# Key units by context half, rounding copies on ScalarE, and NF4 chunks placed 1-8-3 around the attention heads

## The reference

```
def nf4_quant_dequant(w):             # blocks of 64 along a row
    absmax = max(abs(block)); normalized = block / absmax
    idx = searchsorted(bounds, normalized)        # 15 bounds, 16 codes
    return NF4_CODE[idx] * absmax
x = x + attention(layernorm(x), ctx, ctx, mask, Wq, Wk, Wv, Wo)
    # 32 query heads, 8 key/value heads of 128, rotary positions on q and k,
    # logits = 30 * tanh(q k / sqrt(128) / 30), softmax over 128 keys
dq1, dq2, dq3 = (nf4_quant_dequant(w) for w in (w1, w2, w3))   # 1376x512, 1376x512, 512x1376
h = silu(layernorm(x) @ dq1.T) * (layernorm(x) @ dq2.T)
x = x + h @ dq3.T
```

## Time and profile before

| | us |
|---|---|
| median of 3 runs (893.6 to 898.36) | 896.76 |
| the profiled execution | 898.33 |
| its span | 896.4 |
| TensorE busy | 819.5 (91%) |
| VectorE busy | 706.8 (79%) |
| ScalarE busy | 439.3 (49%) |
| GpSimd busy | 467.9 (52%) |

### The profile page before, as it was taken

One profiled execution on the slowest core, in us unless ns is written; L12 is line 12 of the kernel. 1 busy time (PEld: TensorE's weight loads), 2 busy tenths in 40 slices (PEclk: granted clock), 3 DMA queues, 4 the chain that ended last, 5 costly groups with the idle time before them and its releaser, 6 DMA issues.

```text
span 896.4 us, 10644 instructions
## 1 busy us (share of the span) xinstructions
PE 819.5 (91%) x3806; PEld 650.7 (73%) x3806; DVE 706.8 (79%) x793; ACT 439.3 (49%) x521; POOL 467.9 (52%) x272
## 2 busy tenths in 40 slices
PE   3688799899899999899999899999767999998998
PEld 3566587677677778677777677777546788887886
DVE  8798968589888988788888788988887799895120
ACT  0044466466565566555665565565642365462100
POOL 3445437865965955846856847857321335444000
PEclk9899999899999999999999999999989999999999
DMA  8454564632433432522523423422201311303210
GB/s 322 135 156 144 158 202 107 195 113 67 115 113 82 149 83 71 171 60 71 162 74 89 146 63 91 147 71 58 81 1 32 103 48 54 106 1 103 56 59 36
DMA packets 61941, 91.82 MB, mean 102 GB/s; under 512 B 6721, under 2 KB 28353, under 8 KB 61889
## 3 DMA queue, kind: packets, MB, share of 16 engines
q1 hardware_dynamic: 61888, 91.14, 34.6%
HBM read 51.00 MB, written 19.14 MB: 78 GB/s over the span
## 4 chain that ended last, share of the span: by engine, by line
PE 52%; DVE 17%; POOL 13%; DMA 7%; issue 6%; ACT 4%; SPq 2%; POOLq 0%; DVEq 0%; ACTq 0%
POOL qT L1120 6%; PE bank L449 5%; PE bank L450 5%; PE bank L451 5%; PE bank L536 4%; DMA sw<-cs_loop 4%; PE bank L469 3%; PE bank L467 3%; PE bank L468 3%; PE bank L483 3%; PE bank L484 3%; PE bank L485 3%; PE trp L456 3%; PE avp L547 3%; DVE nfa L848 2%
## 5 line engine op out<-in xcount | busy, mean ns | idle before, releaser
L848 DVE SCALAR_TENSOR_TENSOR nfv<-nfp,nfv 128x1408 f32<-128x1408 uint8 x70 | 139.6, 1994 | 24.5 <-ACT nfp L681 22.7
L1120 POOL TENSOR_TENSOR qT<-cs_loop,sw 128x512 f32<-128x512 f32 x58 | 90.5, 1560 | 107.1 <-DMA sw<-cs_loop 102.1
L730 ACT ACTIVATE eb<-bank 128x512 f32<-128x512 f32 x64 | 38.3, 598 | 188.2 <-PE bank L536 188.2
L848 DVE SCALAR_TENSOR_TENSOR nfa<-nfp,nfa 128x1408 f32<-128x1408 uint8 x56 | 104.0, 1857 | 25.0 <-ACT nfp L681 24.4
L1185 POOL TENSOR_TENSOR eb<-eb,maskf 128x512 f32<-128x512 f32 x64 | 91.8, 1435 | 52.1 <-ACT eb L732 52.1
L681 ACT ACTIVATE nfp<-nfv,bnd 128x1408 uint8<-128x1408 f32 x75 | 106.9, 1460 | 14.3 <-DVE nfa L848 9.1
L483 PE MATMUL bank<-woh,ath 128*128 128x512 f32 x256 | 109.5, 428 | 0.0
L681 ACT ACTIVATE nfp<-nfa,bnd 128x1408 uint8<-128x1408 f32 x75 | 106.5, 1461 | 5.6 <-POOL nfa L1136 3.1
L467 PE MATMUL bank<-xh,wqh 128*128 128x512 f32 x256 | 106.8, 417 | 0.0
L848 DVE SCALAR_TENSOR_TENSOR nfx<-nfp,nfx 128x1408 f32<-128x1408 uint8 x42 | 83.7, 1992 | 25.2 <-ACT nfp L681 25.2
L484 PE MATMUL bank<-wol,ath 128*128 128x512 f32 x256 | 102.6, 401 | 0.0
(11 more groups left out here) (130 smaller groups left out, 1835.6 us busy)
## 6 DMA issues: line engine op xcount, KB each, us to landing
sw<-cs_loop SPq DMA_DIRECT2D x116, 128.0 KB, 2.3
stage<-wq_pieces SPq DMA_DIRECT2D x32, 256.0 KB, 2.9
stage<-wo_pieces SPq DMA_DIRECT2D x32, 256.0 KB, 2.9
stage<-dq_scratch SPq DMA_DIRECT2D x32, 256.0 KB, 3.2
sw<-cs_start SPq DMA_DIRECT2D x44, 128.0 KB, 2.4
ks_scratch<-qT SPq DMA_DIRECT2D x16, 256.0 KB, 2.5
vs_scratch<-vst SPq DMA_DIRECT2D x16, 256.0 KB, 3.3
kcur<-ks_scratch SPq DMA_DIRECT2D x16, 256.0 KB, 3.7
```

The source lines that it names most:

```text
L848: op = nc.vector.scalar_tensor_tensor(acc[:, :], nfp[:, n % 2, :], STEPS[i], acc[:, :], ALU.mult, ALU.add)
L1120: nc.gpsimd.tensor_tensor(dst, products(ru, slot)[:, 0, :], sw[:, slot, :], ALU.add).then_inc(roped, 1)
```

## The change

Five things change together.

1. Key units run over all eight key heads for the first half of the tokens, then for the second (`half, kv = u // 8, u % 8`), and Wk comes by head, so that key unit 0 needs piece 0 and context pieces 1 to 4 and starts with the first two; key units 1 to 7 need one piece more each.
2. The casts of pieces 0 to 27 are made by ScalarE (`first_hi`). VectorE and GpSimd share the low halves anew (`FIRST_POOL`). The six first groups of token transposes stand after key units 10 to 15, two after value units 0 and 1.
3. One chunk (the first quarter of w3) is made in value units 0 to 12, eight in the heads, three (45 steps) in hidden units 2 to 21 and behind them. w3 is cut by columns (`W3_RUNS`), so that early tiles of the down product need early chunks only.
4. The cast `hh` goes to ScalarE (`hidden_hi`), for unit n-1 after the silu of n.
5. The down product waits for the hidden low halves tile by tile.

```diff
@@ sync @@
-            for n in range(12):
+            for n in range(5):
                 first_piece(n)
+            sp.dma_start(tab[:, :, :], table_d).then_inc(tab_in, 16)
             sp.dma_start(mt8[:, :], mask_t).then_inc(mask_in, 16)
...
             for v in range(16):
-                if v == 4:
-                    nf_load(nf_first[:, CH:2 * CH], 1)
+                if v == 13:
+                    nf_load(1)
+                if v == 14:
+                    nf_store(0)
                 if v == 5:
-                    nf_store(dq3[:, 0:CH], 0)
...
+            sp.wait_ge(nf_out, nf_stored(NKV))
+            nf_load(NKV + 2)
             for n in range(4, 2 * HT):
-                if n == 14:
-                    nf_load(nf_first[:, 4 * CH:5 * CH], 11)
-                if n == 16:
-                    nf_store(dq3[:, 2 * CH:3 * CH], 10)
+                if n == 15:
+                    nf_store(NKV + 1)
+                if n == 17:
+                    nf_load(NKV + 3)
                 weights_in(n)
@@ tensor @@
+                half, kv = u // 8, u % 8
+                if u > 0:
+                    split(pe, 5 + u if half == 0 else 16)
...
+                for k in range(KT):
+                    if u == 0:
+                        split(pe, k + 2)
...
-                if n == 0:
-                    pe.wait_ge(h_lo, 2 * HT)
+                pe.wait_ge(h_lo, units_of(n))
@@ scalar @@
+            for n in range(16):
+                first_hi(n)
+            for u in range(10, NK):
+                first_token_hi(u - 10)
+                if u >= 12:
+                    first_hi(u + 4)
...
+                if v < 2:
+                    first_token_hi(6 + v)
+                for n in range(20 + 2 * v, 22 + 2 * v) if v < 4 else ():
+                    first_hi(n)
+                for i in nf_values(v):
+                    nf_above_bound(0, i)
...
                 silu(n)
-                chunk, bounds = nf_ffn(n)
-                for i in bounds:
-                    nf_above_bound(chunk, i)
+                if n > 0:
+                    hidden_hi(n - 1)
+                for c, i in nf_ffn(n):
+                    nf_above_bound(NKV + 1 + c, i)
+            hidden_hi(2 * HT - 1)
+            for c, i in nf_ffn(2 * HT):
+                nf_above_bound(NKV + 1 + c, i)
@@ vector @@
             for u in range(NK):
                 rope_parts(u, u % 2, tab[:, 0:2, :])
-                if u < 2:
-                    first_piece(12 + 2 * u)
-                    first_piece(13 + 2 * u)
+                if u < 6:
+                    first_low(5 + 2 * u)
...
-                for i in nf_keys(u):
-                    nf_add(0, i)
...
-                dve.wait_ge(h_done, n + 1)
-                nc.vector.tensor_copy(hh[:, t, half * 512:(half + 1) * 512], hf[:, n % 2, :]).then_inc(h_hi, 1)
...
+                if n in (1, 7, 14):
+                    nf_prepare(NKV + 1 + n // 7)
+                for c, i in nf_ffn(n):
+                    nf_add(NKV + 1 + c, i)
+            for c, i in nf_ffn(2 * HT):
+                nf_add(NKV + 1 + c, i)
@@ gpsimd @@
+                for n in {0: (8,), 2: (10,), 3: (12,), 5: (14,), 12: (16,), 13: (18,)}.get(u, ()):
+                    first_low(n)
-                if u == 2:
+                if u == 5:
                     power(0, range(B))
...
+            first_low(20)
+            nf_normalise(0)
+            for n in (22, 24, 26):
                 first_low(n)
...
+                if u == 3:
+                    nf_rescale(0)
+            nf_normalise(1)
...
-                if n in (1, 10):
-                    nf_normalise(10 + n // 10)
-                if n in (9, 18):
-                    nf_rescale(10 + n // 18)
+                if n in (1, 7, 14):
+                    nf_normalise(NKV + 1 + n // 7)
+                if n in (9, 16):
+                    nf_rescale(NKV + 1 + n // 16)
+            nf_rescale(NKV + 3)
```

More of the change, by code:

```diff
@@ L122, in build @@
         sb("ffn_place", [128, 6144])
+        with ExitStack() as ffn:
+            nfy = sb("nfy", [128, CH], f32, ffn)
         woh1 = sb("woh1", [128, G, D], f32r)
@@ L198, in split @@
         def split(eng, n):
-            if isinstance(n, int) and n <= WO0:
-                wait(eng, piece_lo, (n + 1) // 2)
-                wait(eng, piece_lo_dve, n // 2)
+            if n <= WO0:
+                early_pool = len([m for m in range(n) if m in FIRST_POOL])
+                wait(eng, piece_lo, early_pool)
+                wait(eng, piece_lo_dve, n - early_pool)
             else:
-                eng.wait_ge(piece_lo, n - WO0 // 2)
+                eng.wait_ge(piece_lo, n - WO0 + len(FIRST_POOL))
         def source(n):
@@ L244, in nf_ffn @@
         def nf_ffn(n):
-            chunk, m = (10, n - 2) if n < 10 else (11, n - 11)
-            return chunk, range(15 * m // 8, 15 * (m + 1) // 8) if 0 <= m < 8 else []
+            return [divmod(k, 15) for k in range(45 * (n - 2) // 21, 45 * (n - 1) // 21)] if n >= 2 else []
         def nf_head(kv, b):
-            if kv == 0:
-                return {0: [], 7: [12, 13, 14]}.get(b, [2 * b - 2, 2 * b - 1])
             if kv == NKV - 1:
@@ L396, in head @@
                 if last:
-                    wait(sp, nf_out, 16 * 9)
+                    sp.wait_ge(nf_out, nf_stored(NKV - 1))
                     for n in range(4):
                         weights_in(n)
-                if last:
-                    nf_load(nf_first[:, 3 * CH:4 * CH], kv + 3)
+                    nf_load(NKV + 1)
             def weights_in(n):
@@ L506, in _ @@
                         .then_inc(mask_count, 1)
[L507 to L514 removed]
+                if u >= 10:
+                    first_transposes(u - 10)
             for v in range(16):
@@ L717, in _ @@
                 nc.scalar.activation(vst[:, v % 4, :], prj2[v % 2][:, :], ACT.Copy).then_inc(v_copied, 1)
-                chunk, bounds = nf_values(v)
-                for i in bounds[0:1]:
-                    nf_above_bound(chunk, i)
-                for i in bounds[1:]:
-                    nf_above_bound(chunk, i)
+                if v < 2:
+                    first_token_hi(6 + v)
[3 more added lines that the diff above has]
+                    nf_above_bound(0, i)
                 if 9 <= v < 13:
@@ L978, in _ @@
                     rope_parts(NK + u, u % 2, csq[:, :, :])
-                for i in bounds[1:]:
-                    nf_add(chunk, i)
+            nf_prepare(1)
             def add_out(unit):
@@ L1065, in hidden @@
             def hidden(n):
-                t, half = UNITS[n]
                 dve.wait_ge(silu_done, n + 1)
@@ L1086, in _ @@
                 hidden(n)
-                if n in (1, 10):
-                    nf_prepare(10 + n // 10)
-                chunk, bounds = nf_ffn(n)
-                for i in bounds:
-                    nf_add(chunk, i)
+                if n in (1, 7, 14):
[4 more added lines that the diff above has]
+                nf_add(NKV + 1 + c, i)
             for n in range(HT):
@@ L1147, in nf_rescale @@
                 nf_blocks(nf_bufs(c)[1], nfm[:, c % 2, :]).then_inc(nf_scaled, 1)
-            for n in range(0, 12, 2):
+            for n in (0, 3, 6):
                 first_low(n)
```

300 lines of the change are left out of this document (145 added, 155 removed).

## The result

The changed kernel took 917.06 us (median of 4 runs, 912.64 to 917.73), the kernel before 896.42: a ratio of 1.0222, 95% interval 1.018 to 1.0265 (the front part has three of the four runs of the kernel before, hence 896.76 there). It is slower, as forecast, but by 20.6 us instead of 5, outside the range of 886 to 911 and outside the widest one, 883 to 915. Whether it is over 2% slower the interval leaves open. The profiled execution has a span of 914.8 against 896.4.

The account below looks back on a forecast made before the run. TensorE was taken to bound the FFN with VectorE close behind, and something ahead of TensorE the start. Terms -20 + 4 - 1 + 6.8 + 6.6 + 7.6 + 1 = +5.0 gave 903.3 profiled, 902 median; range 886 to 911, widest 883 to 915.

Parts of the forecast that it names:

- Term 1: The start: earlier first matmul and a faster key chain bring value unit 8 from 114.59 to 94.5; -20 us.
- with 2.8 a unit: Key units: two can't take less than 5.6 us, so the chain was walked at 2.8 each from 23.3.
- Rival 4: Key units get no faster than 3.6 each, from swap waits and low halves; start gain -12, time 910, chance 0.13.
- Term 2: Way into the heads: chunk 0's store delays query unit 4's swap; first weighted values after 11.6 instead of 7.7; +4 us.
- sum 3 at -5.3: Way into the heads: query sum 3 placed 5.3 us before the last query unit's end, then low halves and rescale.
- Term 3: Head 0: its first unit loses a rescale and a normalising, -1 us; the other heads taken as 0.
- the other rhythm: Heads: the prediction falls if the heads, which keep their order, settle in another rhythm.
- Term 4: FFN near hidden unit 2: late cast delays normalising, bounds and weight halves; TensorE idles about 5 us, with clock +6.8.
- term 5: FFN, hidden unit 12: weight piece 15 waits behind the first FFN chunk's store; gap 4 to 5, with clock +6.6.
- term 6: FFN end: bounds and adds precede the first w3 halves, wait 10.9 to 11.5 instead of 3.5; +7.6, plus 1 for clock.
- Rival 1: The FFN takes it: both waits inside the hidden units vanish, only the end's 8 to 9 stays; about 888, chance 0.27.
- VectorE busy over 95% in the hidden units: Hidden units: a sign that the forecast is right, with VectorE's work counted at 115 to 119 us.

Follow-up runs that it names:

- b2: Changed kernel with the x load issued in quarters behind the swaps of key units 0 to 3, chunk 0's load behind that of unit 5; 912.65 us.
- h2: Changed kernel without the first LayerNorm's statistics, constants in their place; 912.27 us.
- h3: Changed kernel with the low halves of pieces 8, 10, 12 and 14 on VectorE instead of GpSimd; 916.23 us.
- b3: Changed kernel with ScalarE's copies of value weight pieces 16 to 19 ahead of the token copies in key units 12 to 15; 917.57 us.
- c_all: Changed kernel with the edits of a1 to a4, b2 and b3, and chunk 1's normalising behind the first two masks; 881.47 us.
- a1: Changed kernel with chunk 0's store issued behind the swaps of early query units 4 and 5 instead of ahead of them; 908.24 us.
- d2: c_all with chunk 1 loaded behind the swaps of early query units 4 and 5, prepared and normalised in head 0, its bounds there as before the change; 886.12 us.
- d1: c_all with chunk 0's fifteen bounds and adds starting in value unit 3 and ending in unit 12, instead of starting in unit 0; 877.46 us.
- a2: Changed kernel with the halves of gate weight pieces 4 and 5 ahead of the first FFN chunk's first two bounds and adds; 910.73 us.
- a3: Changed kernel with the first FFN chunk's store issued ahead of weight piece 17 instead of 15; 912.58 us.
- a4: Changed kernel with the last five bounds and adds behind the halves of w3 tiles 0 and 1 and the next ones, two per tile; 905.20 us.
- d3: Changed kernel with each hidden unit's rounding copy back on VectorE behind its product, instead of on ScalarE; 918.04 us.

## Why the prediction was wrong

**Term 1 (the start, -20) was -11.1: the step that failed is the walk of the chain of key units "with 2.8 a unit", from a first sum that "can't start before 22 or 23" and was taken to end at 23.3.** The runs show 3.13 a unit and an end at 26.4. Value unit 8 was forecast at 94.5 and came at 103.52. The 9.0 in between are four pieces:

- 3.1 for the first sum. That its swap queues behind the bytes of x and NF4 was forecast, and b2 shows it. The size was off: the load of chunk 0, issued at 10.11, took 14.1 to land (12.3 before), and the sum starts 0.9 after that landing. Why the load took longer is not shown. The sum stands at 25.11, before at 25.01, so all of the 7.35 us that TensorE's first matmul had gained is lost here.
- 1.6 from there to unit 12: 41.0 instead of 39.4. Errors hid each other. The pace gives 4.0 more (h2). The low halves at units 0, 2, 3 and 5, for which the walk has 1.8 in all beside its 2.8 a unit and the 4 of the LayerNorm, were free (h3), and the statistics cost 3.4 instead of 4.
- 1.9 before value unit 0. The copy of piece 19 stands behind a token copy; b3 takes 1.1 of this wait away, the rest is not shown.
- 2.4 in the value units, and not by waits: these are 4.6 in all, start to start, where the forecast has 5.3. Value unit 0 took 4.73 where 2.73 was counted, for it ran mostly at the lower of the two clocks (granted 0.50 from 73.9 to 76.6), and the token transposes behind units 0 and 1 were left out of the count. In c_all, after a shorter wait, the same unit took 3.18.

The second matmul of value unit 0 in the changed kernel, where 0.39 is the duration at the higher clock:

```profile
74.49 0.63 PE L464 MATMUL bank<-wcl,cth 128*128 128x512 f32 x1
```

Taking the shortest cycle that the row allows as the mean was the mistake. Rival 4, which gave -12 for this term, was nearer than the forecast. Its condition was 3.6 a unit, with the LayerNorm it was 3.4; of its two reasons the waits for swaps are in the trace, and the low halves cost nothing (h3).

**Term 2 (into the heads, +4) was +8.7.** The mechanism was right: rescale, store in SyncE's queue, swap 4, mask, and a1 takes it away. The size was off at its first link, "sum 3 at -5.3". Two low halves of 1.3 lead from there to "-2.7", so the -5.3 has to be its end; it ended 1.2 ahead of the end of the last query unit and had started 2.4 ahead of TensorE's last matmul. Its swap was issued at 134.25, right behind the 704 KB load of chunk 1, and took 5 us to land (the view of the DMAs has 4.4 as the median of this stretch). With the load moved away (d2) the sum starts 5.9 ahead, with it in its place (c_all) 3.0: the load is worth 2.9. I counted the places of the moved store and forgot the moved load. The other 1.2 or so would be the length of the sum itself, if -5.3 was meant as its start; the prediction doesn't say. The later links are late by 3.9 (rescale) to 4.8 (sum 5 and all behind it).

**Term 3** with the other heads (-1, and 0 for the rest) was -2.2, and that it is near is luck. Head 0, which was to give 1, took 63.7 instead of 63.2. Heads 1 to 6 took 386.4 instead of 391.8, though their order is the same: the other rhythm that the prediction had named as a way to fall. Before, three of these six heads took 67.0 to 67.3, in the changed kernel one. The last head with the way to the hidden units took 2.8 more. In c_all and d1, again with the same order, heads 1 to 6 took 391.9 and 393.2, so this term can't be told from the scatter of the heads.

**Term 4 (+6.8) was +6.5, term 5 (+6.6) +6.8, term 6 with its clock (+8.6) +9.3**, each from the start of the same hidden unit in both traces. In term 6 all 9.3 are the wait; the 1 for the clock was 0, since the matmuls behind the shorter wait before the change ran at the lower clock too (granted 0.65 from 827.1 to 832, and 0.65 from 845.6 to 850 in the changed kernel). Another 0.5 comes from the lower clock in the first hidden matmuls. a2, a3 and a4 take the waits away one by one, and nothing comes in their place. For term 5 the place in SyncE's queue is shown; that the copy on ScalarE makes the rescale late is not, since with the copy on VectorE it is as late (d3). Rival 1 (the FFN takes it) is refuted.

Together: the profiled execution took 916.73 instead of 903.3, 13.4 more. Term 1 makes 8.9 of it and term 2 4.7. Both lie beyond the bounds that the prediction had set for them (-12 and 5), and so the time lies beyond its widest range.

**A reason that was false beside right sizes:** "VectorE busy over 95% in the hidden units". It was 110.16 of 141.8, 78%. The end is long because of the order in two lists, not because VectorE is full; a4 shows it, with the same work and a wait 9.3 shorter. The two lines of the low half on GpSimd, before and after, each from 716 to 824:

```profile
L1222 POOL TENSOR_TENSOR hl<-hf,hh 128x512 fp32r<-128x512 f32 x19 | 41.0, 2157 | 55.7 <-DVE hh L1073 55.7
```

```profile
L1250 POOL TENSOR_TENSOR hl<-hf,hh 128x512 fp32r<-128x512 f32 x17 | 26.1, 1534 | 74.1 <-ACT hh L812 74.1
```

With its input made by ScalarE a subtraction takes 1.53 us instead of 2.16, and the adds took 1.92 in the mean (63.5 us for 33) instead of 2.08. The run d3, with the copy back on VectorE, has 2.20 and 2.16, so the place of the copy makes the difference; that GpSimd now begins in VectorE's pauses more often is my reading of it. The line of d3:

```profile
L1250 POOL TENSOR_TENSOR hl<-hf,hh 128x512 fp32r<-128x512 f32 x16 | 35.1, 2196 | 58.6 <-DVE hh L1099 58.6
```

"SBUF — State Buffer" of the Trainium skill, section "Who interferes with whom", says that VectorE and GpSimd share one pair of ports as an exclusive lock, that a VectorE instruction with two inputs in SBUF contends for it with a GpSimd instruction that reads SBUF, and that ScalarE waits for neither. The rows agree with it: an add takes 1.61 alone and 2.08 to 2.16 in the mean beside the subtractions, a subtraction 1.29 alone and up to 2.6. By that rule I had weighed 5 us more for VectorE's added work; the adds took less time each instead, with the copy on ScalarE.

## What to carry to other kernels

When a store or load is moved in the list of the engine that issues DMAs, ask two things of everything behind it: how long the store's own wait holds it up, and how much longer a small transfer takes with a large one beside it. Waits that come from order in a list, not from work, can be taken away one by one, and here their gains added up (35.9 against 35.6). A cycle time read from one good cycle is a lower bound: take the mean over the stage. And where stages scatter from run to run, as the heads do here, compare a version with more than one profile of the other.

## What the runs showed of the hardware

- Two waits of nearly the same length can cost differently. In the changed kernel TensorE idled 2.48 us before the logits at 498.80, and the transposes behind them took 0.60 for four; in the kernel before it idled 2.42 before 377.13, and they took 1.06:

```profile
498.80 1.12 PE L558 MATMUL bank<-qT,kcur 128*128 128x512 f32 x2 [2.48 <-POOL qT L1149]
499.76 0.60 PE L470 MATMUL trp<-tab,nrm 128*128 128x128 f32 x4
```

```profile
377.13 1.30 PE L536 MATMUL bank<-qT,kcur 128*128 128x512 f32 x2 [2.42 <-POOL qT L1120]
378.22 1.06 PE L456 MATMUL trp<-tab,nrm 128*128 128x128 f32 x4
```

  The granted clock is 1.00 from 495 to 505 in the one, the higher level throughout, and 0.83 from 374 to 384 in the other, a part of it at the lower. Of heads 1 to 6 in the changed kernel, c_all and d1, one with such a wait takes 65.2 to 65.4 us, with the lower clock 66.6 to 67.4, without the wait 63.4 to 63.6; which of them comes differs from head to head and from run to run. What decides it no run shows.
- The 128 KB swap transfers land in 2.4 us in the median; behind x and the first chunk they took 10.8 (3.6 in c_all, with these moved behind them), beside the load of chunk 1 some 5.
